# A recurrence with reordered steps, and an output stage that transposes its attention sums by 32-token blocks

## The reference, cut to what matters

```python
log_D = where(mask, cs[..., :, None] - cs[..., None, :], -inf) + ig[..., None, :]
max_log_D = max(log_D, -1);  D = exp(log_D - max_log_D)
C = (qh @ kh.T / sqrt(64)) * D
h = (C / (maximum(abs(C.sum(-1)), exp(-max_log_D)) + 1e-6)) @ vh
x = x + head_norm(h) * out_w
```

```python
scores = softmax(h @ Wg, -1).transpose(0, 2, 1);  idx = sort(top_k(scores, 2))
q, k, v = per_expert(h[idx])
p = softmax(q @ k.T / 8, axis=1);  ao = (p @ v) @ Wo + bo
outs = zeros.at[idx].add(ao)
x = x + layernorm(h + outs) * ln_g + ln_b
```

## Time and profile before

| | |
|---|---|
| three runs | 1901.15, 1907.59, 1908.03 us; median 1907.59 |
| profiled execution | 1910.44 us; span of the trace 1908.6 us |
| mean granted clock of PE over the span | 0.965 of full speed |
| busy share of the span | PE 87%, DVE 74%, POOL 65%, ACT 57% |
| recurrence | to about 1180 us |
| routing and expert stage | to 1459 us |
| output stage | 1459 us to the end |

### The profile page before, as it was taken

The page is one execution under the profiler, slowest core; times in us unless marked ns, Lnnn a source line. Parts: engine busy times, 40 slices in busy tenths (PEclk is TensorE's granted clock), DMA queues, the critical chain, the costliest instruction groups (busy, mean ns, idle before and its releaser), DMA issues. The chain is left out here.

```text
span 1908.6 us, 58899 instructions
## 1 busy us (share of the span) xinstructions
PE 1664.9 (87%) x22686; PEld 1266.1 (66%) x22845; DVE 1406.2 (74%) x3051; ACT 1092.8 (57%) x2550; POOL 1233.8 (65%) x1218
## 2 busy tenths in 40 slices
PE   4888888998898998898998886899995989899894
PEld 3677777777777777777777774899994444444442
DVE  2577777677777776776777777687753598999998
ACT  3677677776776776676777764223333454454640
POOL 1466776667667667666767666678873475757654
PEclk9899999999999999999999998999997999999997
DMA  6123223222222222222322102755543167676776
GB/s 206 52 85 100 87 85 102 85 91 96 89 87 96 91 95 85 93 94 85 102 85 91 57 35 74 256 149 179 173 140 73 40 147 171 155 173 154 176 177 155
DMA packets 106597, 218.02 MB, mean 114 GB/s; under 512 B 13008, under 2 KB 14416, under 8 KB 105552
## 3 DMA queue, kind: packets, MB, share of 16 engines
q1 hardware_dynamic: 96080, 180.68, 33.0%
q0 software_dynamic: 10240, 33.56, 6.0%
HBM read 147.08 MB, written 67.11 MB: 112 GB/s over the span
## 5 line engine op out<-in xcount | busy, mean ns | idle before, releaser
L318 POOL TENSOR_TENSOR rec_hn<-rec_hn,rec_out_w 128x512 f32<-128x512 f32 x128 | 199.3, 1557 | 213.6 <-DVE rec_hn L739 213.6
L1365 POOL TENSOR_TENSOR out_x_half<-out_x_half,ln_b 128x512 f32<-128x512 f32 x128 | 163.7, 1313 | 152.7 <-DVE out_z_half L1509 152.7
L296 POOL TENSOR_TENSOR rec_hrs<-rec_harg,rec_minus_half 128x8 f32<-128x8 f32 x128 | 213.1, 1664 | 10.0
L1396 ACT ACTIVATE out_ao<-out_o_ps,sigma_rows 128x512 f32<-128x512 f32 x128 | 88.0, 687 | 197.6 <-PE out_o_ps L1451 197.6
L705 DVE TENSOR_TENSOR rec_c<-rec_s_ps,rec_d 128x512 f32<-128x512 f32 x256 | 165.0, 686 | 38.0 <-PE rec_s_ps L426 34.8
L536 ACT ACTIVATE rec_d<-rec_l_ps 128x512 f32<-128x512 f32 x256 | 151.7, 593 | 61.3 <-PE rec_l_ps L450 60.5
L1003 PE MATMUL exp_q_ps<-exp_wqkv,exp_rows_t 128*128 128x192 f32 x1024 | 177.0, 326 | 0.0
L954 POOL DMA_INDIRECT exp_x_rows<-x_scratch,rowid x128 | 136.5, 1066 | 45.5 <-issue 25.0
L1003 PEld LDWEIGHTS exp_q_ps<-exp_wqkv,exp_rows_t 128*128 128x128 f32 x1024 | 165.4, 190 | 0.1
L472 PE MATMUL rec_o_ps<-rec_v_one,rec_c 128*64 128x65 f32 x4096 | 156.0, 231 | 1.4 <-issue 1.0
L1064 ACT ACTIVATE exp_rows_t<-exp_t_ps 128x512 f32<-128x512 f32 x128 | 69.4, 594 | 147.1 <-PE exp_t_ps L991 120.0
(11 more groups left out here) (220 smaller groups left out, 4417.9 us busy)
## 6 DMA issues: line engine op xcount, KB each, us to landing
rec_x_ring<-in_x SPq DMA_DIRECT2D x128, 256.0 KB, 3.0
rec_ctx_ring<-in_ctx SPq DMA_DIRECT2D x128, 256.0 KB, 3.1
x_scratch<-rec_x_ring SPq DMA_DIRECT2D x128, 256.0 KB, 2.0
out_x_half<-x_scratch SPq DMA_DIRECT2D x128, 256.0 KB, 5.6
out<-out_x_half SPq DMA_DIRECT2D x128, 256.0 KB, 4.0
exp_wqkv<-in_wqkv SPq DMA_DIRECT2D x4, 1536.0 KB, 7.4
exp_x_rows<-x_scratch,rowid POOLq DMA_INDIRECT x128
wo<-in_wo SPq DMA_DIRECT2D x1, 2048.0 KB
```

The lines of the kernel that those rows point to most:

```text
L296: nc.gpsimd.tensor_tensor(hrs[:, G % 2], harg[:, G % 2], mhalf[:], ALU.pow).then_inc(hrs_done, 1)
L318: nc.gpsimd.tensor_tensor(h, h, w8[:], ALU.mult).then_inc(hw_done, 1)
L1365: nc.gpsimd.tensor_tensor(xt[H % XR][:, q, :], xt[H % XR][:, q, :], lb[:], ALU.add).then_inc(xb_done, 1)
```

## The change

In the recurrence: the zero matmuls are dropped and the first head pair's state matmuls open the accumulation. The state update matmuls become a function of their own, placed between the two log_decay steps. For the last chunk of a sequence the rows transposes stand behind the products, and the x-hat turn before log_decay. On ACT, log_sigmoid, parts and gate_weights move behind the second decay exponential and the x1 copy. On DVE, the rows copy moves behind the input offsets, residual moves ahead of advance, token_moments ahead of the last gate step, and in the last chunk the router copy behind them.

In the output stage: out_av_t holds one block of 32 positions and is doubled; each block has its own 16 transposes of 32 rows and two copies on ACT, made two blocks ahead. The sums are made in four pieces of 512 columns, three instructions each: on DVE for the first 128 positions, wholly on POOL for the others, one piece in each of four successive halves. The tile of sums is doubled.

```diff
--- before.py
+++ after.py
@@ -115,7 +115,6 @@
...
     ident_bf = sb("ident_bf", [P, P], BF16)
-    zeros = sb("zeros", [P, KC * V], BF16)
     mask_bf = sb("mask_bf", [P, KC, P], BF16)
@@ -252,7 +251,6 @@
...
         nc.gpsimd.memset(rin[:], 0.0)
-        nc.gpsimd.memset(zeros[:], 0.0)
         nc.gpsimd.memset(deps[:], (DH * LN_EPS) ** 0.5 * DEN_EPS)
@@ -457,14 +455,12 @@
...
                 pe.wait_ge(st_done, outer(g - 1))
-                for e in range(2):
-                    nc.tensor.matmul(o_ps[e][:, 0:KC * V], ident_bf[:], zeros[:], start=True, stop=False)
                 for k in range(KC):
...
                             nc.tensor.matmul(o_ps[e][s:s + DH, k * V:(k + 1) * V], qe[g % 2][r, k, s:s + DH],
-                                             state[r, k, :], start=False, stop=False)
+                                             state[r, k, :], start=(k == 0), stop=False)
             for e in range(2):
@@ -473,30 +469,38 @@
...
             mm.then_inc(o_full, 1)
-            if c < NC - 1:
-                pe.wait_ge(kw_done, outer(g))
-                after(pe, st_done, outer(g) - 1)
-                for k in range(KC):
-                    for e in range(2):
-                        h = 2 * k + e
-                        mm = nc.tensor.matmul(u_ps[DH * e:DH * (e + 1), k * V:(k + 1) * V], kw[:, outer(g) % 2, h, :],
-                                              v1[:, g % VR, h, :], start=True, stop=True)
-                mm.then_inc(u_full, 1)
+
+        def updates(g):
+            pe.wait_ge(kw_done, outer(g))
+            after(pe, st_done, outer(g) - 1)
+            for k in range(KC):
+                for e in range(2):
+                    h = 2 * k + e
+                    mm = nc.tensor.matmul(u_ps[DH * e:DH * (e + 1), k * V:(k + 1) * V], kw[:, outer(g) % 2, h, :],
+                                          v1[:, g % VR, h, :], start=True, stop=True)
+            mm.then_inc(u_full, 1)

         for g in steps:
+            last = g % 4 == 3
             if valid(g):
...
                 turn_ctx(g + 8)
-            if valid(g + 1) and (g + 1) % 4:
+            if valid(g + 1) and not last:
                 log_inter(g + 1)
-            if order.gate_key(g, 0):
+            if order.gate_key(g, 0) and not last:
                 gate_group(order.gate_key(g, 0))
...
                 products(g)
+            if order.gate_key(g, 0) and last:
+                gate_group(order.gate_key(g, 0))
+            if valid(g + 8) and last:
+                turn_hat(g + 8)
             if valid(g + 1):
                 log_decay(g + 1, 0)
-            if valid(g + 8):
+            if valid(g) and not last:
+                updates(g)
+            if valid(g + 8) and not last:
                 turn_hat(g + 8)
@@ -646,17 +650,17 @@
...
                 normalise(g + 9)
-            if 0 <= n < nb and g % 4 == 0:
-                log_sigmoid(n)
-            if 0 <= n < nb and g % 4 == 2:
-                gate_weights(n)
-                parts(n, 0)
             if valid(g + 10) and g % 2 == 0:
...
                 put_x1(g - 3)
+            if 0 <= n < nb and g % 4 == 0:
+                log_sigmoid(n)
+            if 0 <= n < nb and g % 4 == 2:
+                parts(n, 0)
+                gate_weights(n)
             if valid(g - 4) and g % 4 == 3:
@@ -807,7 +811,7 @@
...
                 weigh(g, 1)
-            if order.gate_key(g, 0):
+            if order.gate_key(g, 0) and g % 4 < 3:
                 gate_step(order.gate_key(g, 0))
@@ -819,18 +823,22 @@
...
                 input_offsets(g + 9)
+            if order.gate_key(g, 0) and g % 4 == 3:
+                gate_step(order.gate_key(g, 0))
+            if valid(g - 2):
+                residual(g - 2)
             if valid(g) and g % 4 < 3:
                 advance(g)
-            if order.gate_key(g, 1):
+            if order.gate_key(g, 1) and g % 4 < 3:
                 gate_step(order.gate_key(g, 1))
...
                 input_moments(g + 11)
-            if valid(g - 2):
-                residual(g - 2)
+            if valid(g - 3):
+                token_moments(g - 3)
+            if order.gate_key(g, 1) and g % 4 == 3:
+                gate_step(order.gate_key(g, 1))
             if order.gate_key(g, 2):
                 gate_step(order.gate_key(g, 2))
-            if valid(g - 3):
-                token_moments(g - 3)

@@ -1287,9 +1295,9 @@
...
     mhalf = sb("mhalf", [P, 4])
-    t1 = sb("part1", [P, NE, DH])
-    av = [sb(f"av{i}", [P, NE, DH]) for i in range(2)]
-    avz = sb("av_t", [P, HP, P, 2, 2])
+    t1 = sb("part1", [P, NE // 2, DH])
+    av = [[sb(f"av{p}{i}", [P, NE, DH]) for i in range(2)] for p in range(2)]
+    avz = [sb(f"av_t{b}", [P, HP, 32, 2, 2]) for b in range(2)]
     ao = [sb(f"ao{b}", [P, HP, E]) for b in range(2)]
@@ -1342,23 +1350,31 @@
...
     def _(pool):
-        nc.gpsimd.memset(avz[:], 0.0)
+        for b in range(2):
+            nc.gpsimd.memset(avz[b][:], 0.0)
         nc.gpsimd.memset(ones[:], 1.0)
...

-        def attend(c):
-            p = att[:, c, :].rearrange("p (h i j) -> p h i j", i=2, j=2)
-            for i in range(2):
-                if c or i:
-                    pool.wait_ge(av_done, 2 * c + i)
-                nc.gpsimd.tensor_tensor(t1[:], vall[:, c, :, 1, :], p[:, :, i, 1].unsqueeze(2).broadcast_to([P, NE, DH]),
-                                        ALU.mult).then_inc(t1_done, 1)
-                pool.wait_ge(t1_done, 2 * c + i + 1)
-                pool.wait_ge(t0_done, 2 * c + i + 1)
-                nc.gpsimd.tensor_tensor(av[i][:], av[i][:], t1[:], ALU.add).then_inc(av_done, 1)
-
-        attend(0)
+        def attend(c, n):
+            i, q = divmod(n, 2)
+            hs = slice(8 * q, 8 * q + 8)
+            p = att[:, c, :].rearrange("p (h i j) -> p h i j", i=2, j=2)[:, hs, i]
+            dst = av[c % 2][i][:, hs, :]
+            full = [P, NE // 2, DH]
+            if n == 0:
+                after(pool, at_full, 4 * (c - 1))
+            pool.wait_ge(av_done, 4 * c + n)
+            nc.gpsimd.tensor_tensor(dst, vall[:, c, hs, 0, :], p[:, :, 0].unsqueeze(2).broadcast_to(full), ALU.mult
+                                    ).then_inc(t0_done, 1)
+            nc.gpsimd.tensor_tensor(t1[:], vall[:, c, hs, 1, :], p[:, :, 1].unsqueeze(2).broadcast_to(full), ALU.mult
+                                    ).then_inc(t1_done, 1)
+            pool.wait_ge(t0_done, 4 * c + n + 1)
+            pool.wait_ge(t1_done, 4 * c + n + 1)
+            nc.gpsimd.tensor_tensor(dst, dst, t1[:], ALU.add).then_inc(av_done, 1)
+
+        for n in range(2):
+            attend(1, n)
         for H in range(HALVES):
@@ -1369,24 +1385,23 @@
...
             nc.gpsimd.tensor_tensor(rs[H % 2][:], ve[H % 2][:], mhalf[:], ALU.pow).then_inc(rs_done, 1)
-            if H % 8 == 3 and H // 8 + 1 < NC:
-                attend(H // 8 + 1)
+            c, n = divmod(H + 2, 8)
+            if n < 4 and c + 1 < NC:
+                attend(c + 1, n)

...

-        def spread(c):
-            for n in range(4):
-                i, q = n // 2, n % 2
-                act.wait_ge(at_full, 4 * c + n + 1)
-                if n == 0 and c:
-                    act.wait_ge(o_full, 8 * 4 * c)
-                for e in range(2):
-                    r = slice(DH * e, DH * (e + 1))
-                    ins = nc.scalar.activation(avz[r, 4 * q:4 * q + 4, :, e, i],
-                                               t_ps[n % 2][r].rearrange("p (h b) -> p h b", h=4), ACT.Copy)
-                ins.then_inc(at_read, 1)
+        def spread(B):
+            act.wait_ge(at_full, B + 1)
+            if B >= 2:
+                act.wait_ge(o_full, 8 * (B - 1))
+            for e in range(2):
+                r = slice(DH * e, DH * (e + 1))
+                ins = nc.scalar.activation(avz[B % 2][r, :, :, e, :],
+                                           t_ps[B % 2][r].rearrange("p (h i b) -> p h b i", h=HP, i=2), ACT.Copy)
+            ins.then_inc(at_read, 1)

@@ -1412,43 +1427,44 @@
...
             evict(0, hp)
+        spread(1)
         for H in range(HALVES):
             B, m = divmod(H, 2)
-            if H % 8 == 6 and B // 4 + 1 < NC:
-                spread(B // 4 + 1)
             if B + 1 < NBLK:
...
                     evict(B + 1, hp)
+            if m == 0 and B + 2 < NBLK:
+                spread(B + 2)

...

-        def av_transposes(c):
+        def av_transposes(B):
+            c, rows = B // 4, slice(32 * (B % 4), 32 * (B % 4) + 32)
+            after(pe, at_read, B - 1)
             for n in range(4):
-                i, q = n // 2, n % 2
-                pe.wait_ge(av_done, 2 * c + i + 1)
-                if 4 * c + n >= 2:
-                    pe.wait_ge(at_read, 4 * c + n - 1)
-                for m in range(4):
-                    hp = 4 * q + m
-                    mm = nc.tensor.transpose(t_ps[n % 2][:, m * P:(m + 1) * P],
```

(51 more changed lines are left out.)

## The result

The two kernels, run in turn on one chip, took:

| | before | after |
|---|---|---|
| median of 4 runs | 1907.81 us (1901.15 to 1909.69) | 1853.58 us (1849.96 to 1856.25) |
| ratio | 1 | 0.9721 [0.9691, 0.9751] |
| span of the profiled execution | 1908.6 us | 1854.4 us |
| mean granted clock | 0.965 | 0.977 |

What follows compares the result with a forecast made beforehand. PE sets the pace, with waits in the recurrence. Recurrence: -31.7 - 93.7 + 35 + 11 - 7 = -86 us; output stage -19; in all -105, so 1805 us profiled, 1803 us median, range 1768 to 1850 us.

Steps and rivals of the forecast that it cites:

- The output stage: Output stage: boundaries -23.3, earlier start -6.8, transposes +5.6 and contention +5 give -19 us.
- The transposes: Output stage: 16 small transposes before the first half of 14 blocks, +0.4 us net each, +5.6 us.
- The contention: Output stage: POOL attention slows DVE's two-input instructions by 2.1 us a half; two runs of four halves cost +5 us.
- the 23.3 us that went: Output stage: the three attention chunks in mid-stage cost PE 7.8 us each, and this goes: -23.3 us.
- Zeros: Recurrence, PE: dropping two zero matmuls before the state product saves 0.33 us in 96 chunks, -31.7 us.
- rival (1): DVE and POOL take over the recurrence's pace: recurrence -45 us, output stage as forecast, 1844 us; chance 0.22.
- Rival (4): Zeros' time is waited away before the state matmul, as qe or state sum arrives unchanged: 1835 us; chance 0.08.
- Rows step: Recurrence, fourth chunk: row transposes' wait for POOL goes; the later DVE row copy stalls decay matmuls 1.1 us a period, +35.
- The cumulative sum, +11: Recurrence, second chunk: the later sigmoid chain delays POOL's addition, so PE waits 0.35 us a period, +11 us.
- The clock, -7: Recurrence: half of the 15 us lost to clock dips comes back as their longest wait goes, -7 us.
- moved behind the copy, it leaves the wait for the x1 copy without a cause: Recurrence, ACT: moving the sigmoid chain behind the x1 copy ends the context transposes' wait, 24.1 us in 900, -29.7 us.
- cover the exponential in between: Recurrence, PE: updates between the two decay products, 0.8 us of work, hide the wait for ACT, 17.5 us in 900.

Runs made afterwards that it cites:

- the residual late: The changed kernel with residual put back behind input_moments on the vector engine: 1829.21 us, 0.9588 of the kernel before.
- the three edits: The kernel before with only the rows step moved, the zero matmuls dropped and the new output stage: 1824.92 us, 0.9563.
- cutting the chain at either end: The changed kernel with input_variances behind the x1 copy on ACT, 1830.44 us, or with residual behind input_moments on DVE, 1829.21 us.
- Taking that part away: Kernel before with rows step moved, zeros dropped, new output stage and DVE's new order, plus input_variances behind the x1 copy: 1836.43 us, 0.9623.

## Why the prediction was half right

**The output stage: right in its total, with two terms off that cancel.** -18.6 us in the profile and -17 alone, -19 forecast. The transposes cost less than their term: blocks without attention pieces take 1470.25 - 1446.31 = 23.94 us, 0.13 more than before, not 0.4; the 14 of L1454 fill only 0.85 us to the next product, 0.06 each. The contention costs more: 15 such blocks would be 359.1 us, and the last starts at 369.2, so 10 us, not 5; 1.7 of them are one z product of 8.85 us in place of 7.15, in a stretch where the clock reads 0.86 (1576 to 1588 us). The clock has a part in the 23.3 us that went, too, which the prediction put down to the pieces of attention alone: at the three boundaries before, stretches of 12 us read 0.72, then 0.95 and 0.90, then 0.86, which is 7 us at most. ACT's copies out of PSUM take 0.63 us each and not the 1.09 taken over from the earlier trace rows; ACT has room here, so this costs and gives nothing. The halves with pieces, DVE first, then POOL:

```profile
1547.11 5.34 DVE L1545 SCALAR_TENSOR_TENSOR out_z_half<-out_z_half,out_agg,ln_g 128x512 f32<-128x512 f32 x4
```

```profile
1546.72 1.39 POOL L1368 TENSOR_TENSOR out_av<-v_all,att 128x512 f32<-128x512 f32 x1
1548.07 1.50 POOL L1370 TENSOR_TENSOR out_part<-v_all,att 128x512 f32<-128x512 f32 x1
1549.71 1.53 POOL L1374 TENSOR_TENSOR out_av<-out_av,out_part 128x512 f32<-128x512 f32 x1
```

Four DVE instructions take 5.34 us where they took 2.73: 2.6 us a half, against 2.1 forecast. The halves come 1568.43 - 1554.99 = 13.4 us apart, not 11.9. POOL's three take 4.4 us, not 3.1. The count of two runs of four halves, and DVE as the engine that falls behind, held. By the rule of the Trainium skill (SBUF — State Buffer, section Who interferes with whom) whoever starts second is blocked for the other's whole instruction; here DVE lost 2.6 us and POOL 1.3 over my estimate for it, so the trace agrees in kind: both lose, each for a part.

**Zeros: nearly right alone, wrong in the sum.** -31.7 forecast, -27 alone, -9 on top of the rows step. Before the change PE's idle time elsewhere left DVE room; with each of PE's waits gone, DVE's lateness shows in more places (the row copy, 12 us), and the clock's gain can be had only once. This is rival (1), the one nearest to what came: it had the recurrence at -45 and the kernel at 1844 us. Rival (4) had the zeros' saving eaten by the query product or the state sum; neither is waited for.

**Rows step: better than forecast.** -42.5 with +35 for the copy that was to come late next. The copy costs 8.8 us in 850, 11 in the recurrence, and in the kernel with this step alone nothing. I had taken 1.1 us a period, between 0.65 and 1.6. Where the residual is late again the same place reads (PE):

```profile
649.86 1.16 PE L424 MATMUL rec_s_ps<-rec_q_t,rec_k_t 64*128 64x128 f32 x16
...
654.61 0.39 PE L445 MATMUL rec_l_ps<-rec_mask_bf,rec_ident_bf 128*128 128x512 bf16 x1 [0.29 <-DVE rec_rows L803]
```

The decay matmul starts 654.61 - 649.86 = 4.75 us after the scores, as counted for the copy (4.7). But PE has work until 4.75 - 0.29 = 4.46 us, where I had counted 4.05, and in no period does the contended head norm stand in the way (the longest wait is 0.5 us). The cumulative sum, +11, costs about half of that, though no idle time is listed for it. In the changed kernel PE's first matmul of it follows POOL's log forget gates at once and stands 647.97 - 647.73 = 0.24 us behind the matmul before it:

```profile
647.57 0.25 POOL L301 TENSOR_TENSOR rec_log_f<-rec_neg_f,rec_ln_f 128x32 f32<-128x32 f32 x1 [1.03 <-ACT rec_ln_f L621]
647.73 0.22 PE L436 MATMUL rec_l_ps<-rec_rows,rec_sel_q 128*128 128x128 bf16 x1
647.97 0.38 PE L387 MATMUL rec_sm_ps<-rec_log_f,rec_triu 128*128 128x32 f32 x2
```

Before, it stood 0.06 us behind it in every period, so 0.18 us a period are lost, 6 us in the recurrence. The mechanism was the forecast one (0.35 us a period). The clock, -7, gives about twice that: the dips went altogether, though other waits (up to 0.9 us) stayed.

**The step that failed: "moved behind the copy, it leaves the wait for the x1 copy without a cause".** The sigmoid chain was a cause and its removal works: with the residual late the wait is 0.4 us, and on top of the three edits ACT's order takes 23.5 us of it down to nothing. But the same change put the residual, which waits for POOL, ahead of the input moments on DVE, and the input variance that waits for these moments stands ahead of the x1 copy on ACT. I asked only who waits for the state sum behind the residual (3.4 us of cover, which held: nothing waits for it), and costed the later input statistics at nothing, because SP waits on them two chunks and more ahead. The data were not needed soon, but ACT, which stops for them, was. Forecast -29.7, measured +5 (27.7 x 1072.4 / 850 = 34.9 us, before 29.7); cutting the chain at either end gives 23 to 25 us.

**The second failed term: the updates "cover the exponential in between".** They do, and the wait of 21.5 us is gone; but in that place the same matmuls take 0.29 us a chunk longer, 28 us. I priced a move of PE work at nothing.

**The sum.** Zeros -31.7, rows wait -42.5, exponential -21.5 and the updates' place +28, cumulative sum +6, x1 copy +5, clock -15, and the four DVE waits 28.1 x 1072.4 / 850 = +35: -37 us, where 35.6 were measured. That it comes so near is partly luck, as the listed idle times leave out what lies under the counted end of a matmul, and the 15 us of the clock are counted as if PE had been busy through every dip. The DVE order costs 10.5 us on top of the three edits, less than the 23 to 25 that the residual's place costs in the changed kernel. The waits fit: with the sigmoid chain still in front, ACT waits for the input statistics once a period (11.8 us in 850) and not twice (24.7). Taking that part away gives nothing there, because the late input variance holds up POOL and with it the cumulative sum.

## What to carry to other kernels

When a step that waits is moved ahead on an in-order engine, follow every instruction behind it to the engine that consumes it, and ask what is queued behind that consumer, even where its data are not needed for long. Savings on the engine that sets the pace do not simply add: each one makes another engine's lateness show (here the row copy and the masked scores of DVE), so price a list of edits as one, by how late the next engine is when all are in. Where a wait seems to cost nothing, compare the distances of start times before and after: the idle times listed leave out what is shorter than the counted end of the matmul before. Of a reordering, try the parts alone: here three of six gave 84 us and a fourth 5.5, and the other two, DVE's order and the updates' place, took some 34 us of it back.
